# First batch's layer 1 made plain, W1's block sums made later from a second load, all sums on VectorE

## The chip, the cores and the metric

The kernel runs on one core of one Trainium2 chip. The metric is the device time of one execution in microseconds (us), the median of several. Shorter is better. The engines are TensorE (PE, matrix products), VectorE (DVE), ScalarE (ACT), GpSimd (POOL) and SyncE (SP, which issues all DMAs here).

## The reference

x is 16 batches of 512 tokens by 512 features. Each batch goes through two layers with a residual, and one of 8 experts is chosen per batch for the last 128 of 512 output columns:

```
h        = gelu(x @ W1 + b1)                 # 512 -> 2048, exact gelu
shared   = h @ W2 + b2                       # 2048 -> 384
expert   = h @ We[index] + be[index]         # 2048 -> 128
out      = x + concat(shared, expert)
```

Everything is float32.

## The kernel before

Every float32 matrix is scaled by a power of two that fits its largest entry and split into a high and a low half in float16 (`..._hi`, `..._lo`). A product is three matmuls: hi x hi, hi x lo, lo x hi (`product`, L845 to L847). ACT makes a high half (a Copy with a scale), DVE the low one (`split_lo`, L553, scalar_tensor_tensor). DVE takes the maxima (`top`, L539); a matmul with ones (`total`, L907) brings a maximum to all partitions, and a few one-column operations (`power`, L544 to L549) make the scale from it.

The hidden dimension is cut in D = 4 groups d of 512 (C = 4 tiles of 128). Layer 1 of a group is a product of 2 x 2 blocks made the Strassen way, with seven block products P1, P2, P6, P5, P7, P4, P3 in that order, each 12 matmuls of 256 columns. They need sums of W1's blocks (`add_s`, four of 128x512 for each group) and of X's blocks (`add_t`, four of 128x512 for each batch, into `t_sum`). Both are made by POOL (L303, L311). Behind three of the products ACT copies a bank (`keep`, L426) and DVE adds another bank to it (`c11` L704, `c22` L711, `c12` L717); then ACT applies the GELU (`gelus`, L434, L440, L445). PE's next products wait for these copies and sums: P6, P7 and P4 for the copies, P3 for c22.

Layer 2 of a group is 16 units of three matmuls of 512 columns (`layer2`), 12 for W2 and 4 for the expert. In `step(b, d)` the seven products of batch b and the 16 units of the group two steps back are interleaved (`UNITS`). Each engine has an order of work written out by hand, `batch` and `closing`, run in a loop over the batches. `closing(b)`, in step d = 3, prepares batch b + 1: its maximum, scales and X splits.

Batch 0 has an order of its own. X's four quarters and W1's four groups are loaded, W2's four groups and the expert's weights behind them. W1's group 0 is split one block at a time (`first_w1_split`), the others in two pieces of 3 and 4 blocks (`w1_split`): the blocks themselves and their sums. The raw blocks lie in places that are free then (slots of `h_ring`, half of `x_raw`, `t_sum`), and their sums in others (slots of `h_ring`, half of `u`). So SP issues W1's last group only when X is split (37.09 us), and W2's groups 2 and 3 behind that. PE does `layer1(0, 0)` to `layer1(0, 2)` without layer 2, then `layer2(0, 0)`, then `layer1(0, 3)` with `layer2(0, 1)` between its products. Layer 2 of groups 2 and 3 falls in steps 0 and 1 of batch 1.

Of the kernel before, what the change touches and what calls it, by code (L numbers as in the profile page):

```python
# [4 lines left out]

# [5 lines left out]
P = 128  # L11
B, N, IN, HID, OUT = 16, 512, 512, 2048, 512
# [8 lines left out]
D = 4  # L21
# [17 lines left out]
W_OP = {P1: 0, P2: 1, P6: 4, P5: 3, P7: 5, P4: 2, P3: 6}  # L39
# [4 lines left out]
S_READY = {P5: 1, P6: 2, P7: 3, P3: 4}  # L44
# [6 lines left out]
W2_READY = (1, 3, 4, 2)  # L51
# [6 lines left out]
def build(nc, x, idx, w1, w2, we, b1, b2, be, out):  # L58
    with ExitStack() as ctx:
# [13 lines left out]
        w2_stage = sb("w2_stage", [P, 2, C * SHARED], F32)  # L73
# [49 lines left out]
        w1_loaded = [sem(f"w1_loaded{d}") for d in range(D)]  # L123
        w2_loaded = [sem(f"w2_loaded{d}") for d in range(D)]
# [27 lines left out]
        s_added = sem("s_added")  # L152
        x_hi_done = sem("x_hi_done")
        x_lo_done = sem("x_lo_done")
        w1_hi_done = sem("w1_hi_done")
        w1_lo_done = sem("w1_lo_done")
        first_w1_hi = sem("first_w1_hi")
        first_w1_lo = sem("first_w1_lo")
# [6 lines left out]

        l1_done = sem("l1_done")
# [22 lines left out]
        def s_sum(d):  # L189

            return u[:, 1].rearrange("p c n -> p (c n)") if d == 1 else h_slot({0: 3, 2: 0, 3: 3}[d])

        def w2_raw(d):
            return w2_stage[:, d] if d < 2 else h_slot({2: 2, 3: 1}[d])[:, :C * SHARED]
# [10 lines left out]
        def w_operand(d, i):  # L205

            k = W_OP[i]
            if k < 3:
                return w1_raw(d)[:, (k + 1) * BLOCK:(k + 2) * BLOCK]
            return s_sum(d)[:, (k - 3) * BLOCK:(k - 2) * BLOCK]  # L210
# [5 lines left out]
        def group_free(engine, b, d):  # L216

            if d < D - 1:
                engine.wait_ge(l2_done, (D - 1) * b + d + 1)
            else:  # L220
                engine.wait_ge(out_summed, OT * b + OT)

# [3 lines left out]
        def _(sp):  # L226
# [30 lines left out]

            for k in range(KC):
                sp.dma_start(x_raw[:, 0, k], x[0, :, k]).then_inc(first_x_loaded[k], 16)
# [9 lines left out]
            sp.wait_ge(x_lo_done, OPS)  # L269
            load_w1(3)  # L270

            sp.wait_ge(first_w1_lo, OPS)
            load_w2(2)

            sp.wait_ge(w1_lo_done, 2)
            load_w2(3)
# [5 lines left out]
            with sp.Fori(0, B // 2 - 1) as pair:  # L282
                for par in (0, 1):
                    b = 2 * pair + par
                    store(b, par, 0)
                    store(b, par, 1)
                    reload_x(b + 2, par, 0)
                    store(b, par, 2)
                    reload_x(b + 2, par, 1)
                    store(b, par, 3)  # L290
                    reload_x(b + 2, par, 2)
                    reload_x(b + 2, par, 3)
                    load_expert(b + 2, par, D * b + 2 * D)
# [6 lines left out]
        @block.gpsimd  # L300
        def _(pool):
            def subtract(to, a, b):
                return nc.gpsimd.tensor_tensor(to, a, b, ALU.subtract)  # L303

            def add_s(d, part):

                a21, a11, a12, a22 = (w1_raw(d)[:, k * BLOCK:(k + 1) * BLOCK] for k in range(4))
                s1, s2, s3, s4 = (s_sum(d)[:, k * BLOCK:(k + 1) * BLOCK] for k in range(4))
                if part == 0:
                    pool.wait_ge(w1_loaded[d], 16)  # L310
                    nc.gpsimd.tensor_tensor(s1, a21, a22, ALU.add).then_inc(s_added, 1)  # L311
                    pool.wait_ge(s_added, 4 * d + 1)
                    subtract(s2, s1, a11).then_inc(s_added, 1)
                elif part == 1:
                    subtract(s3, a11, a21).then_inc(s_added, 1)
                else:
                    pool.wait_ge(s_added, 4 * d + 3)
                    subtract(s4, a12, s2).then_inc(s_added, 1)

            def add_t(b, par, part):  # L320

                b11, b12, b21, b22 = (x_block(par, k, n) for k in (0, 1) for n in (0, 1))
                if part == 0:
                    subtract(t_sum[:, 1], b12, b11).then_inc(t_added, 1)
                    pool.wait_ge(t_added, 4 * b + 1)
                    if b == 0:
                        for k in (KH, KH + 1):
                            pool.wait_ge(first_x_loaded[k], 16)
                    subtract(t_sum[:, 0], b22, t_sum[:, 1]).then_inc(t_added, 1)
                elif part == 1:  # L330
                    subtract(t_sum[:, 2], b22, b12).then_inc(t_added, 1)
                else:
                    pool.wait_ge(t_added, 4 * b + 3)
                    subtract(t_sum[:, 3], b21, t_sum[:, 0]).then_inc(t_added, 1)

            for k in range(KH):
                pool.wait_ge(first_x_loaded[k], 16)
            for part in range(3):
                add_t(0, 0, part)
                add_s(0, part)  # L340
            for d in range(1, D):
                if d == D - 1:

                    pool.wait_ge(first_w1_lo, OPS)
                for part in range(3):
                    add_s(d, part)

            pool.wait_ge(w1_lo_done, 2 * D - 2)
            for b in range(1, B):
                pool.wait_ge(x_loaded[b % 2], 64 * ((b + 1) // 2))  # L350

                pool.wait_ge(x_lo_done, OPS * b)
                for part in range(3):
                    add_t(b, b % 2, part)

        @block.scalar
        def _(act):
            def x_split(b, par, i):
                if i in T_OF:
                    act.wait_ge(t_added, 4 * b + T_READY[i])  # L360
                if not (isinstance(b, int) and b == 0):

                    act.wait_ge(l1_done, OPS * (D * b - 1) + i + 1)
# [4 lines left out]
            def first_w1_split(i):  # L368
                act.wait_ge(w1_scaled, 1)
                if i in S_READY:  # L370
                    act.wait_ge(s_added, S_READY[i])
                nc.scalar.activation(flat(w1_hi, 0, W_OP[i], 1), w_operand(0, i), ACT.Copy,
                                     scale=w1_scale[:, 0:1]).then_inc(first_w1_hi, 1)

            def w1_split(d, sums):
                act.wait_ge(w1_scaled, d + 1)
                if sums:
                    act.wait_ge(s_added, 4 * d + 4)
                    nc.scalar.activation(flat(w1_hi, d, 3, 4), s_sum(d), ACT.Copy,
                                         scale=w1_scale[:, d:d + 1]).then_inc(w1_hi_done, 1)  # L380
                else:
                    nc.scalar.activation(flat(w1_hi, d, 0, 3), w1_raw(d)[:, BLOCK:], ACT.Copy,
                                         scale=w1_scale[:, d:d + 1]).then_inc(w1_hi_done, 1)

            def first_h_split(d):
                act.wait_ge(first_h_scaled, 1)
                act.wait_ge(gelu_done, d + 1)

                if d == 0:
                    act.wait_ge(w1_lo_done, 4)  # L390
                else:
                    act.wait_ge(w2_lo_done, 2)
                nc.scalar.activation(h_ring[:, d, 0], u[:, d].rearrange("p c n -> p (c n)"), ACT.Copy,  # L393
# [15 lines left out]
            def residual(b, par):  # L409

                act.wait_ge(x_lo_done, OPS * (b + 1))
# [6 lines left out]
            def keep(b, d, k):  # L418

                s = D * b + d  # L420
                first = isinstance(b, int) and s == 0
                act.wait_ge(l1_done, OPS * s + 2 * k + 1)
                if not first:

                    act.wait_ge((c11_added, c12_added, c22_added)[k], s)
                nc.scalar.activation(kept[:, k], banks[:, BANK_A], ACT.Copy).then_inc(copies_done, 1)  # L426

            def gelus(b, par, d):
                s = D * b + d
# [6 lines left out]
                if not (isinstance(b, int) and s < 2):  # L436

                    act.wait_ge(h_lo_done, s - 1)
# [10 lines left out]
            def batch(b, par, last=False):  # L449
# [9 lines left out]
                keep(b, 1, 2)  # L459
                gelus(b, par, 1)  # L460
# [5 lines left out]
                keep(b, 2, 2)  # L466
                gelus(b, par, 2)
# [21 lines left out]
            for i in (P1, P2, P6, P5):  # L489
                x_split(0, 0, i)  # L490
            for i in (P1, P2, P6, P5):
                first_w1_split(i)
            keep(0, 0, 0)
            for i in (P7, P4):
# [529 lines left out]
```

## Time and profile before

| what | value |
|---|---|
| median of 3 runs | 1320.81 us (1319.52 to 1322.43) |
| the profiled execution's own time | 1322.36 us |
| its span, first to last instruction | 1320.5 us |
| PE busy | 1278.3 us, 97% |
| DVE busy | 673.5 us, 51% |
| ACT busy | 512.4 us, 39% |
| POOL busy | 114.1 us, 9% |
| mean granted PE clock | 0.987 |

The profile is one execution. Busy time of PE counts matmuls whose ends are modelled. An idle time in brackets is that of the engine just before the instruction, with what released it. The clock is in parts of full speed: 1.00 is 2.4 GHz and 0.50 is 1.2 GHz.

### The profile page before, as it was taken

The numbers are of one execution on the slowest core, as the hardware profiler recorded it, in microseconds if no ns is written. First come the engines' busy times: TensorE is split into PE (matmuls) and PEld (weight loads), VectorE is DVE, ScalarE is ACT, GpSimd is POOL, SyncE is SP. The second block draws the span as 40 slices with busy tenths as digits, with TensorE's granted clock in tenths as the row PEclk, the third lists the DMA queues.
The fourth block names the chain that finished last, engine by engine and source line by source line (L and its number), as shares of the span: only waits on it lengthen the run. The fifth ranks groups of instructions, "written<-read, shape, count | busy, mean of one in ns | idle before, by whom it ended". The sixth has DMA issues, their size and how long they took to land.

```text
span 1320.5 us, 21658 instructions
## 1 busy us (share of the span) xinstructions
PE 1278.3 (97%) x8531; PEld 836.1 (63%) x8531; DVE 673.5 (51%) x805; ACT 512.4 (39%) x837; POOL 114.1 (9%) x84
## 2 busy tenths in 40 slices
PE   5668999999999999999999999999999999999998
PEld 3535666666666666666666666666666666666664
DVE  7776455454545536445544644554454553545442
ACT  3563343343433343433343343334343443334331
POOL 7111010100101010010101001010010101001000
PEclk8888999999999999999999999999999999999999
DMA  5300120102001021110202011020210202021000
GB/s 207 112 1 32 34 64 8 56 32 63 32 23 43 29 64 32 48 47 8 56 32 64 32 40 56 8 56 32 64 32 24 60 15 61 32 58 38 17 17 32
DMA packets 24501, 57.98 MB, mean 44 GB/s; under 512 B 5024, under 2 KB 5024, under 8 KB 21920
## 3 DMA queue, kind: packets, MB, share of 16 engines
q1 hardware_dynamic: 24480, 57.70, 13.8%
q8 instruction: 13, 0.21, 0.1%
q14 instruction: 8, 0.07, 0.0%
HBM read 40.91 MB, written 16.78 MB: 44 GB/s over the span
## 4 chain that ended last, share of the span: by engine, by line
PE 92%; DVE 5%; ACT 1%; issue 1%; ACTq 0%; DVEq 0%
PE out_ps L845 16%; PE out_ps L847 16%; PE out_ps L846 16%; PE banks L845 14%; PE banks L846 14%; PE banks L847 14%; DVE w_lo L553 2%; DVE w_max L539 1%; PE out_ps L969 1%; DVE x_lo L553 1%; DVE h_ring L553 0%; ACT h_ring L393 0%; DVE e_lo L553 0%; ACT w_hi L398 0%; ACT u L445 0%
## 5 line engine op out<-in xcount | busy, mean ns | idle before, releaser
L845 PE MATMUL banks<-x_hi,w_hi 128*128 128x256 f16 x1792 | 492.4, 275 | 24.0 <-ACT kept L426 10.8
L846 PE MATMUL banks<-x_lo,w_hi 128*128 128x256 f16 x1792 | 492.4, 275 | 0.0
L847 PE MATMUL banks<-x_hi,w_lo 128*128 128x256 f16 x1792 | 492.2, 275 | 0.0
L845 PE MATMUL out_ps<-h_ring,w_hi 128*128 128x512 f16 x768 | 292.3, 381 | 10.2 <-DVE w_lo L553 10.2
L846 PE MATMUL out_ps<-h_ring,w_hi 128*128 128x512 f16 x768 | 292.5, 381 | 0.0
L847 PE MATMUL out_ps<-h_ring,w_lo 128*128 128x512 f16 x768 | 292.5, 381 | 0.0
L426 ACT ACTIVATE kept<-banks 128x512 f32<-128x512 f32 x192 | 113.3, 590 | 381.8 <-PE banks L847 381.8
L845 PEld LDWEIGHTS banks<-x_hi,w_hi 128*128 128x128 f16 x1792 | 176.7, 99 | 95.5 <-DVE w_lo L553 10.4
L846 PEld LDWEIGHTS banks<-x_lo,w_hi 128*128 128x128 f16 x1792 | 176.6, 99 | 66.9 <-issue 0.6
L847 PEld LDWEIGHTS banks<-x_hi,w_lo 128*128 128x128 f16 x1792 | 176.8, 99 | 21.6
L711 DVE TENSOR_TENSOR u<-banks,kept 128x512 f32<-128x512 f32 x64 | 44.2, 691 | 273.4 <-ACT kept L426 273.4
L445 ACT ACTIVATE u<-u,b_sb,undo 128x512 f32<-128x512 f32 x128 | 97.2, 806 | 185.1 <-DVE u L717 185.1
L717 DVE TENSOR_TENSOR u<-banks,kept 128x512 f32<-128x512 f32 x64 | 44.2, 691 | 221.8 <-PE banks L847 221.8
L553 DVE SCALAR_TENSOR_TENSOR h_ring<-u,scale,h_ring 128x2048 f16<-128x2048 f32 x64 | 150.5, 2351 | 7.6 <-ACT h_ring L393 5.4
L303 POOL TENSOR_TENSOR t_sum<-x_raw 128x512 f32<-128x512 f32 x32 | 47.3, 1479 | 1065.6 <-DMA x_raw<-x_dram 1018.2
L847 PEld LDWEIGHTS out_ps<-h_ring,w_lo 128*128 128x128 f16 x768 | 75.4, 98 | 91.5 <-issue 1.6
L845 PEld LDWEIGHTS out_ps<-h_ring,w_hi 128*128 128x128 f16 x768 | 75.4, 98 | 62.7 <-issue 11.6
L846 PEld LDWEIGHTS out_ps<-h_ring,w_hi 128*128 128x128 f16 x768 | 75.2, 98 | 51.6 <-issue 0.8
L689 DVE TENSOR_SCALAR h_ring<-u,scale 128x2048 f16<-128x2048 f32 x62 | 79.5, 1282 | 43.6 <-ACT u L445 43.6
L845 PE MATMUL out_ps<-h_ring,e_hi 128*128 128x512 f16 x256 | 97.0, 379 | 0.0
L846 PE MATMUL out_ps<-h_ring,e_hi 128*128 128x512 f16 x256 | 97.0, 379 | 0.0
L847 PE MATMUL out_ps<-h_ring,e_lo 128*128 128x512 f16 x256 | 97.0, 379 | 0.0
(96 smaller groups left out, 878.0 us busy)
## 6 DMA issues: line engine op xcount, KB each, us to landing
x_raw<-x_dram SPq DMA_DIRECT2D x64, 256.0 KB, 3.4
e_raw<-we_dram SPq DMA_DIRECT2D x16, 1024.0 KB, 4.7
out_dram<-x_raw SPq DMA_DIRECT2D x64, 256.0 KB, 2.0
h_ring<-w_dram SPq DMA_DIRECT2D x2, 1024.0 KB, 9.4
w_stage<-w_dram SPq DMA_DIRECT2D x2, 768.0 KB, 13.4
h_ring<-w_dram SPq DMA_DIRECT2D x2, 768.0 KB, 5.1
x_raw<-w_dram SPq DMA_DIRECT2D x1, 1024.0 KB, 11.8
t_sum<-w_dram SPq DMA_DIRECT2D x1, 1024.0 KB, 4.8
```

The source lines that it names most:

```text
L303: return nc.gpsimd.tensor_tensor(to, a, b, ALU.subtract)
L426: nc.scalar.activation(kept[:, k], banks[:, BANK_A], ACT.Copy).then_inc(copies_done, 1)
L445: done = nc.scalar.activation(to[:, j], to[:, j], ACT.Gelu, scale=un, bias=b1_sb[:, C * d + j:C * d + j + 1])
L539: return nc.vector.tensor_reduce(to, of, AX.X, ALU.max, apply_absolute_value=True)
L553: return nc.vector.scalar_tensor_tensor(to, of, s, hi, ALU.mult, ALU.subtract)
L689: nc.vector.tensor_scalar(h_ring[:, d, 0], of, scale[:, par, 1:2], None, ALU.mult).then_inc(h_hi_done, 1)
L711: nc.vector.tensor_tensor(u[:, d % 2, 2:4, NH:], banks[:, BANK_C], kept[:, 2], ALU.add).then_inc(c22_added, 1)
L717: nc.vector.tensor_tensor(u[:, d % 2, 0:2, NH:], banks[:, BANK_C], kept[:, 1], ALU.add).then_inc(c12_added, 1)
L845: nc.tensor.matmul(ps, hi, v_hi, start=start, stop=False, skip_group_check=True)
L846: nc.tensor.matmul(ps, hi, v_lo, start=False, stop=False, skip_group_check=True)
L847: return nc.tensor.matmul(ps, lo, v_hi, start=False, stop=stop, skip_group_check=True)
L969: nc.tensor.matmul(out_ps[:, OT - 1], ones[:, :P], ones[:, :], start=True, stop=True)
```

## The change

Layer 1 of batch 0 is no longer made the Strassen way. `first_layer1(d, c)` makes one tile of 128 hidden features at a time, from 4 x 3 matmuls of 512 columns, into three banks used in turn (`RING`), and ACT applies one GELU to each tile (`first_gelu`). The blocks of W1 are loaded in another order, and split whole (four blocks, group 0 in two halves). X is split in quarters (`first_x_split`), with no sums.

From batch 1 on the Strassen form is as before. It needs the sums of W1's blocks, so W1's four groups are loaded a second time, one after the other, into `stage` (`reload_w1`), summed in place on DVE (`add_s`) and split (`s_split`) over the place of three of the four blocks: group 0 at the end of batch 0's order, groups 1, 2 and 3 in the three first steps of batch 1 (`sums=True`). Batch 1 is therefore taken out of the loops. X's sums (`add_t`) move to DVE too, in each batch behind the splits for P1 and P2. POOL has no work left.

W1's last group and W2's four groups have places of their own from the start (`t_sum`, `stage`, slot 3 of `h_ring`, `kept`), so their first loads wait for nothing.

```diff
-            load_w2(0)
-            load_w2(1)
+            load_w1(3)
+            for d in range(D):
+                load_w2(d)
             load_expert(0, 0)
...
+            sp.wait_ge(w2_lo_done, 2)
+            reload_w1(0)
             load_expert(1, 1, D)
...
+            reload_w1(1)
+            reload_w1(2)
...
+            reload_w1(3)
...
+            def reload_w1(d):
+                if d > 0:
+                    sp.wait_ge(s_lo_done, d)
+                sp.dma_start(s_sum, w1[d]).then_inc(w1_reloaded, 16)
...
+            def first_gelu(d, c):
+                n = C * d + c
+                act.wait_ge(first_l1_done, n + 1)
+                if d >= 2:
+                    act.wait_ge(h_lo_done, d - 1)
+                nc.scalar.activation(u[:, d % 2, c], banks[:, n % RING].rearrange("p j n -> p (j n)"), ACT.Gelu,
+                                     scale=undo1[:, 0, d:d + 1], bias=b1_sb[:, n:n + 1]).then_inc(first_gelu_done, 1)
...
+            w1_split(3)
+            first_h_split(1)
+            first_gelu(2, 0)
+            first_gelu(2, 1)
+            w2_split(0)
...
+            residual(0, 0)
+            s_split(0)
+            for c in range(C):
+                first_gelu(3, c)
...
+            def add_t(b, par):
+                b11, b12, b21, b22 = (x_block(par, k, n) for k in (0, 1) for n in (0, 1))
...
+                nc.vector.tensor_tensor(t_sum[:, 1], b12, b11, ALU.subtract).then_inc(t_added, 1)
...
+            def add_s(d):
+                a11, a12, a22, a21 = (s_sum[:, k * BLOCK:(k + 1) * BLOCK] for k in range(4))
...
+                nc.vector.tensor_tensor(a22, a21, a22, ALU.add).then_inc(s_added, 1)
...
             def batch(b, par, loads=None, sums=False):
                 e_top(b)
+                if sums:
+                    add_s(1)
                 c22(b, 0)
                 c12(b, 0)
+                if sums:
+                    s_split(1)
...
                     x_split(b + 1, 1 - par, P1)
                     x_split(b + 1, 1 - par, P2)
+                    add_t(b + 1, 1 - par)
                 e_split(b, 3)
                 c22(b, 3)
...
+            first_x_split(0)
+            first_x_split(1)
             w1_top(0)
+            first_x_split(2)
+            first_x_split(3)
             w1_scales(0)
+            w1_split(0, 0, 2)
+            w1_split(0, 2, 2)
             w1_top(1)
+            w1_top(2)
             w1_scales(1)
             w1_top(3)
             first_h_top()
+            w1_split(1)
             w1_scales(2)
             w1_scales(3)
             first_h_scale()
+            w2_top(0)
+            w1_split(2)
+            w2_top(1)
             h_split(0, 0, 0)
             w2_top(2)
             w2_top(3)
             e_top(0)
+            w1_split(3)
             w2_scales()
             e_scales(0, 0)
+            h_split(0, 0, 1)
             w2_split(0)
             e_split(0, 0)
             w2_split(1)
             e_split(0, 1)
+            x_top(1, 1, 1)
+            add_t(1, 1)
+            h_split(0, 0, 2)
+            for d in (2, 3):
+                w2_split(d)
+                e_split(0, d)
+            add_s(0)
+            x_scales(1, 1)
+            s_split(0)
+            for i in range(OPS):
+                x_split(1, 1, i)
+            batch(1, 1, 1, sums=True)
...
+            def first_layer1(d, c):
+                n, i, j = C * d + c, c // 2, c % 2
...
+                if n >= RING:
+                    pe.wait_ge(first_gelu_done, n - RING + 1)
+                for k in range(KC):
...
+                    last = product(banks[:, n % RING].rearrange("p j n -> p (j n)"), w1_hi[:, d, op, kc, j],
+                                   w1_lo[:, d, op, kc, j], first_x[0][:, k], first_x[1][:, k], k == 0, k == KC - 1)
+                last.then_inc(first_l1_done, 1)
...
+            def first_batch():
+                for c in range(C):
+                    first_layer1(0, c)
+                    if c == 1:
                         w1_total(1, 1)
+                x_total(0)
+                w1_total(2, 2)
+                for c in range(C):
+                    first_layer1(1, c)
+                for c in range(C):
+                    first_layer1(2, c)
+                    if c == 1:
+                        e_total(0)
+                        pe.wait_ge(w2_max_done, D)
+                        total(w2_tops, w_max[:, D:2 * D]).then_inc(w2_all_done, 1)
                 for unit in range(OT * C):
                     layer2(0, 0, unit, True)
+                x_total(1)
+                for c in range(C):
+                    first_layer1(3, c)
+                for unit in range(OT * C):
+                    layer2(0, 1, unit, True)
```

## Rows read from the trace of the kernel before

**Rows 1.** The page: busy us, share of the span, instructions

```profile
PE 1278.3 (97%) x8531; PEld 836.1 (63%) x8531; DVE 673.5 (51%) x805; ACT 512.4 (39%) x837; POOL 114.1 (9%) x84
```

**Rows 2.** Windows: length, busy us (count) by engine, clock, DMA share, GB/s

```profile
20.00:124.00 104.00, 72.60 (x440) 46.40 (x441) 79.12 (x88) 51.33 (x66) 26.55 (x16) 0.86 0.14 48
124.00:202.00 78.00, 78.00 (x531) 51.58 (x530) 38.42 (x47) 30.23 (x52) 5.54 (x4) 1.00 0.14 41
```

**Rows 3.** Timeline of PE: start us, us, engine, line, what, idle before

```profile
20.04 0.40 PE L845 MATMUL banks<-x_hi,w_hi 128*128 128x256 f16 x1 [2.95 <-DVE w_lo L553]
...
62.99 0.27 PE L845 MATMUL banks<-x_hi,w_hi 128*128 128x256 f16 x1 [1.98 <-ACT kept L426]
...
112.43 0.40 PE L845 MATMUL banks<-x_hi,w_hi 128*128 128x256 f16 x1 [3.63 <-ACT kept L426]
...
123.17 0.38 PE L845 MATMUL out_ps<-h_ring,e_hi 128*128 128x512 f16 x1
...
123.82 0.27 PE L845 MATMUL banks<-x_hi,w_hi 128*128 128x256 f16 x1
...
1316.85 0.38 PE L847 MATMUL out_ps<-h_ring,e_lo 128*128 128x512 f16 x1
```

**Rows 4.** Timeline of DVE, the same maximum in two batches that follow one another

```profile
678.98 2.28 DVE L539 TENSOR_REDUCE e_max<-e_raw 128x1 bf16<-128x2048 f32 x1
...
757.15 2.28 DVE L539 TENSOR_REDUCE e_max<-e_raw 128x1 bf16<-128x2048 f32 x1
```

**Rows 5.** Waits of PE from 0 to 112 us: total, times, longest

```profile
PE out_ps L845 <- DVE w_lo L553: 10.2, 2, 7.6
PE banks L845 <- DVE w_lo L553: 9.0, 5, 3.1
PE banks L845 <- ACT kept L426: 7.2, 5, 2.2
```

**Rows 6.** Timeline of the first 40 us, DVE and POOL

```profile
30.79 1.59 POOL L303 TENSOR_TENSOR h_ring<-x_raw,h_ring 128x512 f32<-128x512 f32 x1
31.18 1.75 DVE L553 SCALAR_TENSOR_TENSOR w_lo<-h_ring,w_scale,w_hi 128x512 f16<-128x512 f32 x1
...
33.51 0.74 DVE L553 SCALAR_TENSOR_TENSOR w_lo<-h_ring,w_scale,w_hi 128x512 f16<-128x512 f32 x1
```

**Rows 7.** Groups by form, 0 to 124 us: busy us, mean ns, idle before

```profile
L553 DVE SCALAR_TENSOR_TENSOR h_ring<-u,scale,h_ring 128x2048 f16<-128x2048 f32 x3 | 7.1, 2352 | 5.4 <-ACT h_ring L393 5.4
...
L445 ACT ACTIVATE u<-u,b_sb,undo 128x512 f32<-128x512 f32 x7 | 5.4, 807 | 9.3 <-DVE u L717 9.3
...
L539 DVE TENSOR_REDUCE w_max<-h_ring 128x1 bf16<-128x2048 f32 x2 | 4.5, 2275 | 0.0
...
L365 ACT ACTIVATE x_hi<-t_sum,scale 128x512 f16<-128x512 f32 x6 | 4.1, 709 | 0.0
...
L379 ACT ACTIVATE w_hi<-h_ring,w_scale 128x2048 f16<-128x2048 f32 x2 | 4.0, 1988 | 0.0
...
L689 DVE TENSOR_SCALAR h_ring<-u,scale 128x2048 f16<-128x2048 f32 x1 | 1.3, 1276 | 0.0
```

**Rows 8.** Windows of batch 0, columns as in rows 2

```profile
16.00:20.00 4.00, 0.19 (x1) 0.10 (x1) 2.86 (x7) 2.19 (x4) 4.00 (x4) 0.50 0.98 404
...
22.00:24.00 2.00, 2.00 (x16) 1.55 (x14) 2.00 (x2) 1.18 (x3) 2.00 (x2) 0.79 0.00 0
...
64.00:67.00 3.00, 3.00 (x16) 2.13 (x15) 3.00 (x3) 0.60 (x1) 0.00 (x0) 0.50 0.01 3
...
112.00:118.00 6.00, 5.57 (x21) 3.07 (x22) 3.49 (x6) 3.78 (x7) 0.00 (x0) 0.50 0.48 175
```

**Rows 9.** Timelines of DVE and PE in step 3 of a batch

```profile
742.86 0.69 DVE L711 TENSOR_TENSOR u<-banks,kept 128x512 f32<-128x512 f32 x1 [2.48 <-ACT kept L426]
...
746.57 0.27 PE L845 MATMUL banks<-x_hi,w_hi 128*128 128x256 f16 x1
```

**Rows 10.** DMA issues: KB each, us from issue to landing

```profile
t_sum<-w_dram SPq DMA_DIRECT2D x1, 1024.0 KB, 4.8
```

More of the change, by code:

```diff
@@ L280, in _ @@
                 load_x(1, 1, k)
+            sp.wait_ge(w2_lo_done, 2)
+            reload_w1(0)
             load_expert(1, 1, D)
[L282 to L293, printed above, removed]
+            reload_w1(1)
+            reload_w1(2)
+            store(0, 0, 0)
+            store(0, 0, 1)
+            reload_x(2, 0, 0)
+            store(0, 0, 2)
+            reload_x(2, 0, 1)
+            reload_w1(3)
+            store(0, 0, 3)
+            reload_x(2, 0, 2)
+            reload_x(2, 0, 3)
+            load_expert(2, 0, 2 * D)
+            with sp.Fori(0, B // 2 - 2) as pair:
+                for par in (1, 0):
+                    turn(2 * pair + 2 - par, par)
+            turn(B - 3, 1)
             for b in (B - 2, B - 1):
@@ L298, in _ @@
                 sp.wait_ge(out_stored[o], 16 * B)
[L300 to L354, printed above, removed]
@@ L356, in _, with first_x_split @@
         @block.scalar
         def _(act):
+            def first_x_split(k):
+                act.wait_ge(x_scaled, 1)
+                nc.scalar.activation(first_x[0][:, k], x_raw[:, 0, k], ACT.Copy,
+                                     scale=scale[:, 0, 0:1]).then_inc(first_x_hi, 1)
             def x_split(b, par, i):
                 if i in T_OF:
-                    act.wait_ge(t_added, 4 * b + T_READY[i])
-                if not (isinstance(b, int) and b == 0):
-                    act.wait_ge(l1_done, OPS * (D * b - 1) + i + 1)
+                    act.wait_ge(t_added, 4 * (b - 1) + T_READY[i])
+                if isinstance(b, int) and b == 1:
+                    act.wait_ge(first_l1_done, HT)
+                else:
+                    act.wait_ge(l1_done, OPS * (strassen(b, 0) - 1) + i + 1)
@@ L409, in residual @@
             def residual(b, par):
-                act.wait_ge(x_lo_done, OPS * (b + 1))
+                if isinstance(b, int) and b == 0:
+                    act.wait_ge(first_x_lo, KC)
+                    act.wait_ge(b2_loaded, 16)
+                else:
+                    act.wait_ge(x_lo_done, OPS * b)
                 act.wait_ge(e_loaded, 32 * (b + 1))
@@ L447, in gelus, with batch @@
                 done.then_inc(gelu_done, 1)
-            def batch(b, par, last=False):
+            def batch(b, par, last=False, sums=False):
                 keep(b, 0, 0)
@@ L466, in batch @@
                 keep(b, 2, 2)
+                if sums:
+                    s_split(3)
                 gelus(b, par, 2)
@@ L521, in _ @@
-            first_h_split(1)
-            w1_split(3, False)
-            w1_split(3, True)
+            first_gelu(2, 2)
+            first_gelu(2, 3)
             w2_split(1)
             e_split(0, 1)
-            w2_split(2)
-            act.wait_ge(b2_loaded, 16)
+            first_h_split(2)
+            for d in (2, 3):
+                w2_split(d)
+                e_split(0, d)
             residual(0, 0)
-            e_split(0, 2)
-            closing(0, 0, False)
-            with act.Fori(0, B // 2 - 1) as pair:
-                batch(2 * pair + 1, 1)
+            s_split(0)
@@ L533, in _ @@
+            for c in range(C):
+                first_gelu(3, c)
+            for i in (P1, P2):
+                x_split(1, 1, i)
+            first_h_split(3)
+            for i in (P6, P5, P7, P4, P3):
+                x_split(1, 1, i)
+            batch(1, 1, sums=True)
+            with act.Fori(0, B // 2 - 2) as pair:
                 batch(2 * pair + 2, 0)
+                batch(2 * pair + 3, 1)
+            batch(B - 2, 0)
             batch(B - 1, 1, last=True)
@@ L725, in finish, with batch @@
                                                ALU.mult, ALU.add).then_inc(out_ready, 1)
-            def batch(b, par, loads=None):
+            def batch(b, par, loads=None, sums=False):
                 h_split(b - 1, 1 - par, 3)
@@ L731, in batch @@
                 e_top(b)
+                if sums:
+                    add_s(1)
                 c22(b, 0)
                 c12(b, 0)
+                if sums:
+                    s_split(1)
                 h_split(b, par, 0)
@@ L739, in batch @@
                 e_split(b, 0)
+                if sums:
+                    add_s(2)
                 c22(b, 1)
@@ L744, in batch @@
                 finish(b - 1, 1 - par, 2)
+                if sums:
+                    s_split(2)
                 h_split(b, par, 1)
@@ L748, in batch @@
                 c11(b, 2)
+                if sums:
+                    add_s(3)
                 c22(b, 2)
@@ L751, in batch @@
                 c12(b, 2)
-                closing(b, par, loads)
-            def closing(b, par, loads):
+                if sums:
+                    s_split(3)
                 if loads is not None:
@@ L825, in _ @@
-            h_split(0, 0, 1)
-            w1_split(3, False)
-            w1_split(3, True)
             w2_split(1)
             e_split(0, 1)
-            w2_split(2)
-            e_split(0, 2)
-            closing(0, 0, 1)
-            with dve.Fori(0, B // 2 - 1) as pair:
-                batch(2 * pair + 1, 1, pair + 1)
+            x_top(1, 1, 1)
+            add_t(1, 1)
+            h_split(0, 0, 2)
+            for d in (2, 3):
+                w2_split(d)
+                e_split(0, d)
@@ L974, in _ @@
             w1_total(0, 1)
-            first_steps()
+            first_batch()
             pe.wait_ge(w2_lo_done, D)
-            with pe.Fori(1, B - 1) as b:
+            for d in range(D):
+                step(1, d)
+            with pe.Fori(2, B - 1) as b:
                 for d in range(D):
```

284 lines of the change are left out of this document (121 added, 163 removed).

## The prediction

> **What bounds the kernel now.** I read the page first, then the windows, then PE's timeline and its waits, then the price list. On the page PE is busy 97% of the span, DVE 51%, ACT 39% [rows 1]: PE sets the end. The windows say where the other 3% lie: from 124 us on PE is busy without a hole at clock 1.00, while from 20 to 124 us it is busy 72.6 of 104 us at clock 0.86, with VectorE (DVE) busy 79.1 of the same 104 [rows 2]. PE's timeline gives the border: the first matmul of batch 1 starts at 123.82 with no wait ahead of it, and the last of the kernel at 1316.85 [rows 3]. Between them lie 15 batches of equal length, one per 78.17 us (757.15 - 678.98) [rows 4], and a tail of 96 matmuls: 15 x 78.17 + 96 x 0.216 = 1193.3, and 1317.07 - 1193.3 = 123.8. So whatever the change does to batch 0 moves the end one for one, and whatever it adds behind batch 0 counts only if it makes PE wait. What delays batch 0 is seen in the waits: PE waits for DVE's low halves (w_lo) 19.2 us and for ScalarE's (ACT) bank copies 7.2 [rows 5].
>
> **The start: what becomes shorter.** Four things change together, so I laid batch 0 out anew, engine by engine in the order of the new code. Prices are start to start, some 0.08 below the duration of a row. DVE: a low half of 2048 columns 2.27, of 512 0.67, of 1536 between them, 1.73; a maximum over 2048 2.2, over 1536, by its columns, 1.67. ACT: a high half of 2048 1.9, of 512 0.61, between them by columns; a GELU of 512 0.76 [rows 6, 7]. A matmul of 512 columns 0.216 at full clock (three from 123.17 to 123.82) [rows 3], one of 256 0.109: a batch has 192 and 336 of them, and 78.17 - 192 x 0.216 = 36.7. From one engine to the next 0.12, from PE 0.22.
>
> First, the price of a low half. With POOL at work on its sums the 128x512 split took 1.75, when it was done 0.74 [rows 6]; the change empties POOL, so all are 0.67 apart. The Trainium skill, SBUF — State Buffer, "Who interferes with whom", says that a VectorE instruction with two SBUF inputs and a GpSimd one that reads SBUF exclude each other for a whole instruction; by that the trace agrees. Were the 1.75 due to something else, two splits of 1024 ahead of PE's start would cost some 2.3 us more, and little behind them.
>
> Second, PE's start. X's four halves, W1's first maximum and scale end as before, near 17.8. ACT then makes 1024 columns (1.05) and DVE their low half (1.2, between 0.67 for 512 and 2.27 for 2048): PE starts at 20.4, against 20.04.
>
> Third, PE's work. Layer 1 plain is 16 tiles x 4 x 3 = 192 matmuls of 512 columns, 41.4 us, in place of 336 of 256, 36.7 us: the plain form costs 4.7 us at full clock. Layer 2 ahead of batch 1 is as before 96 matmuls, 20.7 us. What the plain form takes away is the ping-pong with ACT's copies and DVE's sums inside each group (7.2 and, at 112.43, 3.6 us of idle) [rows 3, 5]: each tile needs one GELU three tiles behind.
>
> Fourth, DVE's queue. From 17.3 it has, in order, 1.8 + 2.4 for W1's first half splits and scale, three maxima 6.6, scales 1.7, first_h_top 0.8, first_h_scale 0.5, three splits of W1 6.8, four maxima of W2 6.7, of E 2.2, W2's and E's scales 1.3, three low halves of h 6.8, four of W2 and E 9.6, X's maximum 2.5, add_t and add_s 4 x 0.60 each, x_scales 0.8, s_split 2.3. Only 2.9 us of it go idle, at 26 to 29, where w1_scales(1) waits for a total that stands behind tile 1 on PE.
>
> Laid against one another: tiles 0 to 3 run 20.4 to 33.8; tile 4 waits for w1_split(1) until 34.8 (**0.9**); tiles 4 to 11 run on to 55.5; layer2(0,0) waits for w2_split(0), which stands behind w1_split(3), the scales and h_split(0,0,1) on DVE, until 57.4 (**1.9**), ends 67.7; tiles 12 to 14 to 75.5; tile 15 waits for tile 12's GELU, which stands on ACT behind s_split(0), which waits for add_s(0) (72.5 to 74.9 on DVE), until 77.8 (**2.2**); layer2(0,1) ends at 90.7. X's splits of batch 1 (ACT 81.4 on) are ahead of that. As a sum: 20.4 + 41.4 + 20.7 + 5.0 of waits + 0.3 of totals and rounding + 2.9 for the slow clock = **90.7**, 33.1 before the old 123.8.
>
> The slow clock: after its idle stretch before 20.04 PE ran at half clock until 22.8 (0.79 granted over 22 to 24), 2.8 us, and from 112.43 on for some 6 us [rows 3, 8]. Half of a slow stretch is lost: 1.4 to 3 us; I take 2.9, near the dear end, because PE starts 0.4 later than before and may just miss the early rise. Before, more slow stretches followed in batch 0 (64 to 67 is one) [rows 8]; the new waits are all under 2.3 us, and I count none.
>
> **What is dear or unknown.** A sum of two SBUF tensors on DVE is in no row. The nearest is 0.69 with one input in PSUM, 0.61 start to start [rows 9]; below it 0.32, a quarter of the 1.28 that one-input scaling takes for 2048 columns [rows 7]; above it 0.67 (the split) and, far, POOL's 1.26 [rows 6]. I take 0.60, same engine, same size. Eight stand in DVE's queue ahead of batch 1: 0.32 gives 88.5, 1.26 gives 98 (7.5 later; two waits pass 4 us and the clock falls again). The second load of W1 (4 x 1 MB) lies beside work: reload_w1(0) goes out once w2_split(1) is done, 59.8, and add_s(0) needs it at 72.5; a load of 1 MB took 4.8 us [rows 10]. The first loads are 9 MB; at 400 GB/s [rows 8] the last is there near 29, and W2's are read from 36 on.
>
> **Batch 1** carries three more add_s and s_split: 2.4 + 2.3 on DVE and 1.9 on ACT in each of three steps. They fall into DVE's idle stretches of 3 to 7 us before each c22. ACT's s_split delays the GELU that frees bank A by 1.9 where some 3 us are free. The third, ahead of x_top(2), pushes x_scales, X's splits and the copy that P7 waits for by 2.3, of which 2 are free: 0.3 lost. If the reload is late (it stands behind stores on SP's queue) each us over 3 counts once.
>
> **Batches 2 to 15**: add_t stands before e_split(b,3) and c22(b,3) on DVE, 2.4 us. DVE idles 2.48 before c22 (742.86 to 743.55), and PE starts P3, which needs it, at 746.57 [rows 9]. So 2.4 must fit in 2.48 + 3.02 = 5.5: nothing is lost.
>
> **Sum.** -33.1 + 0.3 = -32.8. The profiled execution took 1322.36 (span 1320.5 and 1.86 around it), which gives 1289.6; it lies 1.55 above the median of 1320.81, so the median becomes **1288.0**.
>
> **Rivals.**
> A, the forecast: batch 1 starts between 86 and 96, time 1283 to 1293. 0.68.
> B, DVE becomes the bound of batch 0: its queue is full from 29 to 77, so each us that I miss there is late at PE in full, and waits of 4 us bring the slow clock back. Before, a wait of 2.0 us that ended at 62.99 was followed by half clock from 64 to 67 [rows 3, 8], 1.5 us lost. At three waits that is 5, with 3 to 7 of missed work: start 96 to 103, time 1293 to 1301. 0.18. The Trainium skill, TensorE: Matmul & The Clock Gate, "HAM oscillation — how this bites in real kernels", has it that a kernel whose matmuls come in bursts with waits between pays the slow start again and again; taken for all three waits that alone is the 5 us, and 1293.
> C, quicker: sums at 0.32 or fewer waits, start 82 to 86, time 1279 to 1283. 0.09.
> D, slower: add_t on DVE holds up c22 and so PE's P3 in each of 14 batches. It begins to cost at 5.5 us for four sums and takes all of 32.8 back at 5.5 + 32.8/14 = 7.8, 1.96 for one. At 2.2 for one the time is 1320.8 - 32.8 + 14 x 3.3 = 1334. Against it: no two-input row of 512 columns is over 1.75, and those had POOL beside them. 0.02; at POOL's 1.26 it costs nothing.
> E, the gain is largely given back in batch 1 (late reloads, crowded ACT), 13 us or more: over 1301. 0.03.
>
> Anything within 0.2% (2.6 us), about what a measurement of this kernel can tell from no change, needs B, D or E at one exact size: 0.01. Range: A and C's and B's inner parts, 1281 to 1298, holds about 0.85.
>
> **What would show it.** In the new trace: PE's first weight matmul near 20.4; DVE splits of 512 at 0.75 everywhere; waits of about 1, 2 and 2 us on PE near 34, 56 and 76; batch 1's first 256-column matmul near 91; batches 78.17 apart from there. DVE's t_sum sums near 0.69 confirm the price. Wrong it is if PE waits over 4 us, if the clock falls again after 27 us, or if the period grows.

## The result, and the profile after

The changed kernel takes 1288.86 us (median of 4, 1288.61 to 1288.96), the kernel before 1321.62 us in the runs beside it. The ratio is 0.9754, 95% interval 0.9737 to 0.9771: 2.5% faster. Forecast were 1288.0 and a range of 1281 to 1298.

The page after, first the busy time by engine, then waits of PE over the first 100 us (total, times, longest):

```profile
PE 1271.1 (99%) x8387; PEld 818.7 (64%) x8387; DVE 691.7 (54%) x860; ACT 505.5 (39%) x812; POOL 0.2 (0%) x4
```

```profile
PE banks L855 <- DVE w_lo L543: 5.0, 2, 4.2
PE banks L855 <- ACT u L412: 2.6, 1, 2.6
PE banks L934 <- DVE w_max L529: 2.2, 1, 2.2
PE out_ps L855 <- DVE w_lo L543: 1.5, 1, 1.5
```

Against [rows 5] the 10.2, 9.0 and 7.2 us have shrunk to single waits, and from 100 us on PE has none. The 4.2 us in the first row are idle time ahead of PE's first weight matmul at 19.88; in [rows 5] 2.95 of the 9.0 are of this kind. The timeline of PE after holds them:

```profile
19.88 0.61 PE L855 MATMUL banks<-x_hi,w_hi 128*128 128x512 f16 x1 [4.21 <-DVE w_lo L543]
...
34.05 0.39 PE L855 MATMUL banks<-x_hi,w_hi 128*128 128x512 f16 x1 [0.84 <-DVE w_lo L543]
...
56.52 0.38 PE L855 MATMUL out_ps<-h_ring,w_hi 128*128 128x512 f16 x1 [1.52 <-DVE w_lo L543]
...
77.41 0.39 PE L855 MATMUL banks<-x_hi,w_hi 128*128 128x512 f16 x1 [2.57 <-ACT u L412]
...
90.36 0.27 PE L855 MATMUL banks<-x_hi,w_hi 128*128 128x256 f16 x1
```

The last of these rows is the first matmul of batch 1. Before it was at 123.82 [rows 3], so batch 0 gives 33.46 us. What lies behind it is of one length: 1287.2 - 90.36 = 1196.84 against 1320.5 - 123.82 = 1196.68. So the gain of the profiled execution lies in batch 0.

Where did it come from? The windows from PE's first weight matmul to batch 1, the kernel before and then the kernel after:

```profile
20.04:123.82 103.78, 72.42 (x439) 46.23 (x440) 79.08 (x88) 51.11 (x66) 26.51 (x16) 0.85 0.14 48
```

```profile
19.88:90.36 70.48, 65.54 (x294) 28.95 (x295) 61.10 (x75) 42.18 (x43) 0.00 (x0) 0.96 0.28 98
```

A sum of three terms explains both. Work at full clock: 36.7 + 20.7 = 57.4 before, 41.4 + 20.7 = 62.1 after. Waits behind the first matmul, added up from PE's timeline: 31.2 before (17 of them), 0.84 + 1.52 + 2.57 = 4.9 after. The rest, 15.2 and 3.5, is mainly matmuls at half clock, with some small totals. So the plain form costs 4.7 us of work, and the waits fall by 26.3 and the slow part by 11.7. This is bookkeeping; which term causes which is for the experiments.

The waits are of two kinds. Of the 31.2 us before, 15.0 were for bank copies, the sums made from them and GELUs (the ping-pong), and 16.2 for low halves of weights, which stand in VectorE's queue; after, 2.6 and 2.4 are left. The same two rows show a second thing that changed: VectorE is busy 61.10 us in batch 0 instead of 79.08, although it took over eight sums. The twelve additions of a bank to its copy are gone (0.68 each), and so are the low halves of most of the sums.

### The profile page after: what moved, and what is told of

Its sections match the earlier page's. It is cut to its first block, busy times and chain, and to the rows that moved or that the text cites. A ratio compares the mean times of both kernels' runs of the same rounds, so it can differ in the third digit from the quotient of the medians.

```text
span 1287.2 us, 21032 instructions
## 1 busy us (share of the span) xinstructions
PE 1271.1 (99%) x8387; PEld 818.7 (64%) x8387; DVE 691.7 (54%) x860; ACT 505.5 (39%) x812; POOL 0.2 (0%) x4
## 4 chain that ended last, share of the span: by engine, by line
PE 97%; DVE 2%; ACT 0%; issue 0%; ACTq 0%
PE out_ps L855 17%; PE out_ps L856 17%; PE out_ps L857 17%; PE banks L855 15%; PE banks L857 15%; PE banks L856 15%; DVE w_lo L543 1%; PE out_ps L990 1%; DVE w_max L529 0%; DVE x_lo L543 0%; DVE h_ring L543 0%; DVE x_max L529 0%; DVE e_lo L543 0%; ACT u L412 0%; ACT w_hi L369 0%
## 5 line engine op out<-in xcount | busy, mean ns | idle before, releaser
L855 PE MATMUL banks<-x_hi,w_hi 128*128 128x256 f16 (+1 forms) x1744 | 483.4, 277 | 7.6 <-DVE w_lo L543 5.0
L856 PE MATMUL banks<-x_lo,w_hi 128*128 128x256 f16 (+1 forms) x1744 | 483.2, 277 | 0.0
L857 PE MATMUL banks<-x_hi,w_lo 128*128 128x256 f16 (+1 forms) x1744 | 483.2, 277 | 0.0
L404 ACT ACTIVATE kept<-banks 128x512 f32<-128x512 f32 x180 | 106.2, 590 | 366.2 <-PE banks L857 366.2
L855 PEld LDWEIGHTS banks<-x_hi,w_hi 128*128 128x128 f16 x1744 | 170.8, 98 | 80.1 <-DVE w_lo L543 5.2
L856 PEld LDWEIGHTS banks<-x_lo,w_hi 128*128 128x128 f16 x1744 | 170.9, 98 | 71.1 <-issue 1.1
L857 PEld LDWEIGHTS banks<-x_hi,w_lo 128*128 128x128 f16 x1744 | 170.9, 98 | 27.4 <-issue 1.4
L720 DVE TENSOR_TENSOR u<-banks,kept 128x512 f32<-128x512 f32 x60 | 41.5, 692 | 234.0 <-ACT kept L404 234.0
L726 DVE TENSOR_TENSOR u<-banks,kept 128x512 f32<-128x512 f32 x60 | 41.5, 692 | 221.9 <-PE banks L857 221.9
L431 ACT ACTIVATE u<-u,b_sb,undo 128x512 f32<-128x512 f32 x120 | 91.1, 806 | 171.3 <-DVE u L726 171.3
L421 ACT ACTIVATE u<-u,b_sb,undo 128x256 f32<-128x256 f32 x120 | 65.3, 591 | 33.9 <-DVE u L720 33.9
```

The lines of the kernel that those rows point to most:

```text
L421: nc.scalar.activation(t, t, ACT.Gelu, scale=un, bias=b1_sb[:, C * d + 2 + j:C * d + 3 + j])
L431: done = nc.scalar.activation(to[:, j], to[:, j], ACT.Gelu, scale=un, bias=b1_sb[:, C * d + j:C * d + j + 1])
L720: nc.vector.tensor_tensor(u[:, d % 2, 2:4, NH:], banks[:, BANK_C], kept[:, 2], ALU.add).then_inc(c22_added, 1)
L726: nc.vector.tensor_tensor(u[:, d % 2, 0:2, NH:], banks[:, BANK_C], kept[:, 1], ALU.add).then_inc(c12_added, 1)
L855: nc.tensor.matmul(ps, hi, v_hi, start=start, stop=False, skip_group_check=True)
L856: nc.tensor.matmul(ps, hi, v_lo, start=False, stop=False, skip_group_check=True)
```

## The experiments

All times are medians, with the ratio to the kernel before where it is of use. The kernel after stands at 1288.9.

### One bank, and two, in place of three

```diff
-RING = 3
+RING = 1
```

> The new kernel, with its 16 plain tiles in one bank instead of three in turn, so that each tile waits for the GELU of the one before it. If the gain comes from PE no longer waiting for another engine between products (my reading), this puts such a wait behind each of 15 tiles: 0.22 + 0.70 + 0.12 = 1.05 us each, more where the GELU stands behind a split of 1.9 us on ScalarE; some of it falls where PE waits anyway. 12 to 22 us slower than the new kernel, 1301 to 1311 us, with slow-clock stretches among it. If the gain came from the staging or from GpSimd's absence, the ring is idle luxury and the time moves by less than 5 us.

1309.81 us (4 runs, 1308.92 to 1309.86), ratio 0.9915 (0.9899 to 0.9932): 20.9 us of the gain are gone. Waits of PE, from 19 us on:

```profile
PE banks L855 <- ACT u L412: 22.6, 14, 9.4
```

Most single waits are 0.84 to 0.96 us, the bare time of a GELU and its signals; two are 1.6 and 1.7, and one is 9.4, where the GELU stands behind s_split(0) on ScalarE and that behind DVE's sums. The products and loads are the same, only the engines' independence was taken back. So waiting for another engine between products is dear here, as read. This prices a ping-pong of this order, not that of the Strassen form, and it says nothing of the 16.2 us of waits for low halves.

With `RING = 2`:

> The new kernel with two banks in turn. A tile takes 2.6 us and a GELU comes 0.3 us after its tile and takes 0.7, so two banks hide it where ScalarE is free, not where the GELU stands behind a split of 1.9 us or an h split: 1 to 5 us slower, 1290 to 1294. Against one bank this tells whether the length or the queueing of the GELU costs.

1293.59 us (1292.94 to 1295.33): 4.7 us slower than with three banks. The usual GELU is hidden by two banks. Nearly the whole difference is one place: the wait of 2.57 is now one of 5.42 us, reached by PE a tile earlier, as the shorter ring would have it, and matmuls at the slow 0.61 us follow it. (The profiled execution is the slowest of the five, 6.4 us above that of the kernel after; 0.6 of it lie in a later start of PE and a longer first slow stretch.)

```profile
78.22 0.61 PE L855 MATMUL banks<-x_hi,w_hi 128*128 128x512 f16 x1 [5.42 <-ACT u L412]
```

So the third bank pays for queueing on ScalarE, not for the length of a GELU.

### The kernel before without GpSimd's sums in batch 0

```diff
-                    nc.gpsimd.tensor_tensor(s1, a21, a22, ALU.add).then_inc(s_added, 1)
+                    nc.gpsimd.memset(s1, 0.5).then_inc(s_added, 1)
```

The same for the other sums of W1's blocks and of batch 0's X, so these sums are left out and the output is another.

> The kernel before, in which GpSimd writes a constant in place of each of W1's block sums and of batch 0's X sums, so these sums are left out and the output is another; everything else has its place and its waits. Some nine splits of 512 columns on VectorE between 12 and 34 us took 1.5 to 1.75 us beside GpSimd and would take 0.67. If GpSimd's work beside VectorE is what made batch 0 long, up to 8 us of it go: 1312 to 1316 us. If the waits between products are the cause, less than 5 us go, since each of them then ends on another wait.

1313.59 us (1311.9 to 1314.36), ratio 0.9941 (0.9924 to 0.9958): 7.7 us faster, the high end. The splits of 512 are at 0.75 throughout, where [rows 6] has 1.75:

```profile
24.79 0.75 DVE L556 SCALAR_TENSOR_TENSOR w_lo<-h_ring,w_scale,w_hi 128x512 f16<-128x512 f32 x1
```

PE starts at 18.76, not 20.04, and batch 0 ends 8.6 us earlier. Behind the first matmul PE's waits for low halves fall from 16.2 to 9.7 us; the longest, 7.57 ahead of layer2(0, 0), is unchanged, and the waits for copies, sums and GELUs are 18.0 instead of 15.0. So GpSimd at VectorE's side is a part of the long batch 0 and not the main one. The 9.7 us vanish only with the new order, in which VectorE has less to do and W2's splits stand elsewhere in its queue. That these two are the reason is read from the timelines; no run changes them alone. This run also takes away what the sums themselves make others wait for, since a constant is written faster than a sum is made, so it bounds the contention from above.

### GpSimd put back beside VectorE in the kernel after

```diff
+            for n in range(20):
+                if n > 0:
+                    pool.wait_ge(noise_done, n)
+                nc.gpsimd.tensor_tensor(noise[:, :, :], x_block(0, n % 2, 0), x_block(0, n % 2, 1), ALU.subtract
+                                        ).then_inc(noise_done, 1)
```

ScalarE's `residual(0, 0)` waits for these operations too, which holds nothing up: it starts at 68.66, and GpSimd is done at 39.95.

> The new kernel with 20 differences of two 128x512 tensors on GpSimd from 8 us on, results unused, as many as the kernel before had there. If VectorE's two-input operations and GpSimd's exclude one another, the splits of 512 take 1.4 to 1.75 us until GpSimd is done near 40 us, and PE's first matmul comes 2 to 3 us later: 2 to 6 us slower, 1291 to 1295. If the old 1.75 us had another cause, nothing changes.

1292.71 us (1291.25 to 1293.81), ratio 0.9782 (0.9766 to 0.9798): 3.85 us slower, in the range. In the timeline, which is of the slowest of the four executions, PE starts 4.1 us later, more than the 2 to 3 expected:

```profile
8.15 31.80 POOL L333 TENSOR_TENSOR noise<-x_raw 128x512 f32<-128x512 f32 x20 [7.70 <-DMA x_raw<-x_dram]
...
12.26 3.41 DVE L556 SCALAR_TENSOR_TENSOR x_lo<-x_raw,scale,x_hi 128x512 f16<-128x512 f32 x2 [0.79 <-ACT x_hi L340]
15.59 2.28 DVE L542 TENSOR_REDUCE w_max<-h_ring 128x1 bf16<-128x2048 f32 x1
17.79 2.57 DVE L556 SCALAR_TENSOR_TENSOR x_lo<-x_raw,scale,x_hi 128x512 f16<-128x512 f32 x2
...
22.14 3.97 DVE L556 SCALAR_TENSOR_TENSOR w_lo<-h_ring,w_scale,w_hi 128x1024 f16<-128x1024 f32 x2 [1.22 <-ACT w_hi L358]
23.96 0.61 PE L868 MATMUL banks<-x_hi,w_hi 128*128 128x512 f16 x1 [5.85 <-DVE w_lo L556]
```

Pairs of splits that take 1.42, 1.41 and 2.48 alone take 3.41, 2.57 and 3.97, and the maximum over 2048 columns, which reads one tensor, still takes 2.28. Two-input operations on the two engines do hold one another up, both ways of asking agree, and the effect on the whole is 3.9 us in one kernel and at most 7.7 in the other. The Trainium skill, SBUF — State Buffer, "Who interferes with whom", says of a VectorE instruction with two SBUF inputs that it contends with a GpSimd one that reads SBUF, and of tensor_reduce on this chip that it never does; these rows agree.

### The kernel before with its clock kept up

Matmuls of ones into a bank that is not in use yet, where PE waits until layer2(0, 0). Another 22, of 512 columns, stand ahead of PE's first weight matmul.

```diff
+            FILL = {0: {P6: 4, P5: 12, P7: 20, P4: 3, P3: 10}, 1: {P1: 3, P6: 14, P4: 8, P3: 6},
+                    2: {P1: 3, P6: 14, P4: 3}}
...
                 for i in range(OPS):
+                    fill(FILL[0].get(i, 0))
                     layer1(0, 0, i)
...
+                fill(60)
```

> The kernel before, with matmuls of ones into an unused bank put where PE waits until layer2(0, 0), so that its clock stays up. Of the slow clock in batch 0 (31 us at half) about 17 lie ahead of 85 us and 9 of these hold real work. If the clock is a cause of the long batch 0, 5 to 9 us go: 1312 to 1316. If PE only waits for VectorE and ScalarE, the faster products end on the same waits: 0 to 3 us faster, 1318 to 1321.

1319.46 us (10 runs, 1318.11 to 1321.02), ratio 0.9986 (0.9976 to 0.9996): 1.8 us faster. The clock stayed up in three of the stretches where the kernel before ran at half, and in the two at 20 and 33 us; the last, from 112 on, is still slow:

```profile
64.00:68.00 4.00, 3.42 (x30) 2.56 (x28) 4.00 (x4) 0.60 (x1) 0.00 (x0) 1.00 0.01 2
80.00:85.00 5.00, 5.00 (x25) 2.25 (x24) 3.04 (x6) 2.46 (x3) 0.00 (x0) 1.00 0.00 0
98.00:102.00 4.00, 4.00 (x26) 2.35 (x25) 4.00 (x3) 0.00 (x0) 3.92 (x2) 1.00 0.02 4
112.00:119.00 7.00, 7.00 (x40) 4.10 (x37) 2.01 (x3) 3.82 (x7) 0.00 (x0) 0.81 0.42 150
```

And yet PE waits elsewhere: the last wait, before P7 in step 3, grew from 3.63 to 5.24. In the stretches that now ran at 1.00 most of the slow part was time in which PE would otherwise have waited; there the slow clock was a companion of the waits, not the cause. The last stretch is not tested by this. No wait of PE follows it before batch 1, so it probably costs its half in full, by an estimate (118.4 - 112.4) / 2 = 3.0 us in the kernel before.

### The old order of the loads

```diff
-            load_w1(3)
-            for d in range(D):
-                load_w2(d)
+            load_w2(0)
+            load_w2(1)
             load_expert(0, 0)
             sp.dma_start(b2_sb[:, :], b2).then_inc(b2_loaded, 16)
+            sp.wait_ge(first_x_lo, KC)
+            load_w1(3)
+            sp.wait_ge(w1_lo_done, 2)
+            load_w2(2)
+            sp.wait_ge(w1_lo_done, 3)
+            load_w2(3)
```

> The new kernel with the old order of loads: W1's last group only when X is split, W2's groups 2 and 3 behind the first splits of W1. The prediction says the early places are worth nothing by themselves, since every load is there some 2 us or more before it is read: within 1 us of the new kernel. If the free places matter, w1_top(3) at 28.6 waits and with it all behind it: 2 to 6 us slower.

1289.26 us (1288.53 to 1291.03): 0.4 slower, within what can be told from none. The free places are worth nothing as earlier loads. Whether they are worth something by letting the splits run in another order was not tried.

### X's sums in the loop

On GpSimd again from batch 2 on:

```diff
+            for b in range(2, B):
...
+                pool.wait_ge(x_loaded[b % 2], 64 * ((b + 1) // 2))
+                pool.wait_ge(x_lo_done, OPS * (b - 1))
+                subtract(t_sum[:, 1], b12, b11).then_inc(t_added, 1)
```

> The new kernel with X's sums for batches 2 to 15 back on GpSimd (batch 1's stay on VectorE). The prediction counts their move as nothing in the loop: same as the new kernel within 0.1%, 1288 to 1290 us, period 78.17. If the move helped (VectorE no longer slowed by GpSimd at its side in every batch) this is slower by 14 times the part that reaches PE; if it hurt, faster.

1289.22 us (1288.73 to 1289.41): 0.4 us from the kernel after, no difference. VectorE leaves these sums out there. One split in each batch is again at 1.7 (1.66 at 377.60), and nobody waits for it.

More sums on VectorE, four and eight extra in each of 14 batches:

```diff
                     dve.wait_ge(x_lo_done, OPS * (b - 1))
+                    for n in range(4):
+                        if n > 0:
+                            dve.wait_ge(extra_done, 4 * (b - 2) + n)
+                        nc.vector.tensor_tensor(t_sum[:, 1], b12, b11, ALU.subtract).then_inc(extra_done, 1)
+                    dve.wait_ge(extra_done, 4 * (b - 2) + 4)
```

> The new kernel, in which VectorE makes the first of X's four sums four times more in batches 2 to 15 (results unchanged). They wait for one another, so some 0.72 each: 2.9 us more ahead of c22, 5.3 in all. The prediction says that PE begins to wait at 5.5 us: within 1.5 us of the new kernel's 1288.9. If VectorE were near its bound in the loop, each us would show 14 times: 1329 us.

1290.49 us (1289.51 to 1291.01): 1.6 slower, just outside the 1.5 that was expected. From batch 1 on PE has one wait, of 1.0 us in batch 1's step 3, and none in the batches behind it. So 5.3 us of sums fit as a rule.

> As the run before, with eight repeats: 5.8 us more, 8.2 in all, 2.6 to 2.9 beyond the 5.5 us. In 14 batches PE's P3 of step 3 waits that long each: 36 to 40 us slower than the new kernel, 1325 to 1329 us, and the batch period grows to 80.9. This is the rival by which the change would have been slower. If the slack is larger than I read it, the time stays near 1289.

1345.36 us (1343.98 to 1346.39), ratio 1.0189 (1.0172 to 1.0206), slower than the kernel before. The waits are there, but 56.5 us is more than the 36 to 40 expected. Waits of PE from 90 us on, and windows of one step 3:

```profile
PE banks L861 <- DVE u L726: 33.3, 14, 3.9
```

```profile
740.00:742.00 2.00, 1.52 (x8) 0.49 (x5) 1.97 (x4) 0.58 (x1) 0.00 (x0) 1.00 0.00 0
742.00:744.00 2.00, 0.22 (x2) 0.21 (x3) 2.00 (x4) 1.00 (x3) 0.00 (x0) 0.98 0.00 0
744.00:746.00 2.00, 2.00 (x12) 1.39 (x10) 1.04 (x2) 1.75 (x4) 0.00 (x0) 0.50 0.65 217
746.00:748.00 2.00, 2.00 (x8) 0.88 (x7) 0.69 (x1) 0.84 (x2) 0.00 (x0) 0.66 0.77 308
```

The first wait is 3.93 us, the other thirteen are 2.25 to 2.31, a little under the 2.6 to 2.9 expected: the sums take 8.35 on VectorE, so the slack is about 6 us, not 5.5. In 12 of the 14 batches 3.4 us at half clock follow (0.50 over two us, 0.66 over two), of which half is lost: 1.7. PE's matmuls behind the wait show both cases, one batch with the slow stretch and one without:

```profile
251.94 0.28 PE L861 MATMUL banks<-x_hi,w_hi 128*128 128x256 f16 x1 [2.25 <-DVE u L726]
334.22 0.31 PE L861 MATMUL banks<-x_hi,w_hi 128*128 128x256 f16 x1 [2.25 <-DVE u L726]
...
498.62 0.28 PE L861 MATMUL banks<-x_hi,w_hi 128*128 128x256 f16 x1 [2.25 <-DVE u L726]
579.22 0.28 PE L861 MATMUL banks<-x_hi,w_hi 128*128 128x256 f16 x1 [2.25 <-DVE u L726]
```

The first two are 82.28 us apart, the last two 80.60, against 78.17 without the extra sums. Twelve times 4.1, twice 2.4 and 1.7 for the longer first wait make 56 of the 56.5 us. Here, with PE bound on both sides of the wait, the slow clock costs in full what it cost nothing in batch 0 of the kernel before.

### The three waits that are left

ScalarE's order, with the GELUs that were ready first:

```diff
-            s_split(0)
-            for c in range(C):
+            for c in range(C - 1):
                 first_gelu(3, c)
+            s_split(0)
+            first_gelu(3, C - 1)
```

> The new kernel with the GELUs of tiles 12 to 14 ahead of s_split(0) in ScalarE's order. The wait of 2.6 us before tile 15 is put down to this order; s_split(0) is ready at 74.6 only and tile 12 was done at 69. The wait goes and nothing behind it is late: 2.3 to 2.6 us faster, 1286.3 to 1286.6. If tile 15 waits for something else, or X's splits then end late, the gain is under 1 us.

1285.60 us (5 runs, 1285.24 to 1286.0), ratio 0.9735 (0.9721 to 0.9748): 3.3 us faster than the kernel after, a little more than expected. The wait before tile 15 is gone from PE's list, and batch 1 starts at 87.39, 3.0 earlier. In the profiled execution PE also started 0.97 later (20.85) and its first slow stretch ended sooner (clock 1.00 again over 24 to 26), some 1.2 us less lost; the two nearly cancel.

The total of W1's second maximum one tile earlier:

```diff
                     first_layer1(0, c)
-                    if c == 1:
+                    if c == 0:
                         w1_total(1, 1)
...
-            first_gelu(0, 1)
             w1_split(1)
+            first_gelu(0, 1)
```

> The new kernel with the total of W1's second maximum behind tile 0 instead of tile 1 on PE, and w1_split(1) ahead of tile 1's GELU on ScalarE. VectorE's only long idle stretch in batch 0 (2.6 us before 28.05) goes. If VectorE's queue sets the waits at 34 and 56.5 us, both shrink to nothing, 0.8 + 1.5: 1.5 to 2.3 us faster, 1286.6 to 1287.4, unless the third wait grows by as much as the tiles come earlier: then 0.

1288.18 us (1287.64 to 1290.35): 0.7 us by the medians, under the 1.5 to 2.3. The five times reach to both sides of the kernel after's, so this cannot be told from no change. VectorE's idle time did not go, it moved on. Its waits in the kernel after and then here, both for a total on PE:

```profile
28.05 0.16 DVE L534 TENSOR_SCALAR w_exps<-banks 128x1 int32<-128x1 int32 x1 [2.64 <-PE banks L934]
```

```profile
33.02 0.16 DVE L534 TENSOR_SCALAR w_exps<-banks 128x1 int32<-128x1 int32 x1 [1.93 <-PE banks L934]
```

The next total, w1_total(2, 2), stands behind tile 3 on PE, so VectorE gains 0.7 net and no more. The wait at 34 is gone, that at 56.5 became 1.91, the third 2.21, and this third one was followed by half clock this time.

> Both edits together. If the three waits are as read, all 4.9 us go: 1284 to 1284.7. If VectorE bounds the rest, the third gain is partly taken back: 1285 to 1287.

1285.45 us (1284.63 to 1286.29), ratio 0.9736 (0.9722 to 0.9749): no different from the first edit alone, so not all 4.9 us go, and the second case of the expectation holds. It is the fastest of all, with `gelu_first`, by over 3 us against the kernel after.

## Why the prediction was right

**The bound.** PE's start and end of batch 0 decide, the rest is fixed. Right: 1196.84 us behind the border against 1196.68.

**PE's start.** Forecast 20.4, measured 19.88 in the profile; between the kernels that start alike it moves from 19.4 to 20.9.

**The waits of the kernel before.** The prediction put 19.2 us of them down to low halves; 2.95 of these lie ahead of PE's first matmul, so 16.2 delay batch 0 behind it. It named only the ping-pong as what the plain form takes away. More than half of what went is waits for low halves (16.2 to 2.4). The laid-out order held this, since it priced VectorE's new queue one by one, but the text of the prediction does not say so.

**The laid-out order.** Batch 1 at 90.7, measured 90.36. The waits were put at 34.8, 57.4 and 77.8 with 0.9, 1.9 and 2.2 us; they are at 34.05, 56.52 and 77.41 with 0.84, 1.52 and 2.57, on the engines named. Prices from start to start and each engine's order were enough, because VectorE is nearly full here. `gelu_first` confirms the third wait's cause by taking it away.

**The price of a sum on VectorE.** Taken 0.60, in no row. Four sums in the kernel after start 0.61 to 0.73 apart, 0.72 where the next waits for the one before. That wait between two instructions of one engine, 0.11 us each, was not in the estimate; eight sums took 0.5 us more in all.

**The slow clock.** Forecast 2.9 us lost. Measured: half clock from PE's start at 19.88 to about 25.5, so 2.8. No later slow stretch, as counted. The rival by which three such stretches return (B) did not come; `total_early`, where one came behind a wait of 2.21, and `sums12`, where twelve came behind waits of mostly 2.25, show it was near. That the wait of 2.57 in the kernel after had none is in part luck.

**GpSimd beside VectorE.** The row of 1.75 against 0.74 was read as contention. Shown by two runs, from both sides. The prediction says that they exclude each other for a whole instruction and that the trace agrees; the trace shows a little less. Side by side VectorE starts a split every 1.67 us (21.58, 23.25, 24.93, 26.61) and GpSimd a sum every 1.68 (four from 21.19 to 27.89), while alone they start 0.67 and 1.23 apart, 1.90 together.

**The loop.** Sums cost nothing at 2.4 us (`pool_t`), little at 5.3 (+1.6 us), and at 8.2 each batch waits. In rival D the threshold of 5.5 was a little low, about 6, and the price beyond it mis-sized: 14 times the excess, where most excesses also call down the slow clock. By an estimate from `sums12` (1.7 in 12 of 14 batches), one sum of 2.2 us would not have given 1334 but some 20 us more.

**Staging.** Early loads were counted as nothing; `late_loads` agrees.

**Batch 1.** 0.3 us forecast, 0.2 measured, which is too little to tell from none.

The sum: -32.8 forecast, -32.8 measured by medians (1288.86 - 1321.62). That both agree to a tenth is luck: the parts are off by up to 0.5 us either way, and the kernel before moves by 3 us between executions.

## What to carry to other kernels

At the start of a kernel the form with the fewest multiplications need not be the quick one: 4.7 us more of PE's work took away 14 of 17 waits on two other engines, and 18 us of VectorE's work. To forecast such a stretch, write out each engine's queue with start-to-start prices and look at who stands behind whom; and when a wait remains, look first whether something ready is queued behind something that isn't. If sums move to a fuller engine, find the idle time ahead of the next operation that PE needs and count how many fit; past it each microsecond of PE idle may cost more than itself (here 56.5 us for 33.3 us of waits).

## What the runs showed of the hardware

- A wait of PE of about 2 us is sometimes followed by 3.4 us at half clock and sometimes not. In the kernel after a wait of 2.57 us left the clock at 1.00; in `total_early` one of 2.21 was followed by 0.58 and 0.56 over two windows of 2 us. In `sums12` thirteen waits of 2.25 to 2.31 us were followed by it eleven times and twice not.
- The first slow stretch varies between executions of nearly the same order: it ended near 22.8 in the kernel before, near 24 in `gelu_first` and `late_loads`, near 25.5 in the kernel after and 26 in `ring2`, worth up to 1.6 us.
- Twenty two-input operations of 128x512 on GpSimd, with VectorE at work for most of them, took 1.59 us each (`pool_noise`); in the kernel before the same operation took 1.26 to 1.27 while VectorE took a maximum or was idle.
